# The drain of a software-pipelined retention stage: masks as in every other group, the input added by TensorE, own orders for the last steps

## The chip, the core and the metric

The kernel runs on one core of one Trainium2 chip. A core has TensorE (PE, matmuls, writes PSUM only), VectorE (DVE), ScalarE (ACT), GpSimd (POOL) and SyncE (SP, issues DMAs). They share the on-chip memories SBUF and PSUM, and each runs its own instruction stream; streams wait for one another through semaphores only. The metric is the device time of one launch in microseconds, smaller is better.

## The reference

The input is `x` of shape (1, 2048, 128), float32. Four blocks follow one another, each `x = x + block(layernorm(x))`: a retention network of 4 layers, a mixture of experts, a convolution and cumulative-sum block, and the mixture of experts again. Only the first block is touched. Cut to what matters, with `LN` the layer norm over 128 features and 8 heads of 16 features:

```
X = LN(x)
for i in range(4):
    Z = LN(X)
    Q, K, V, G = rotate(Z @ Wq[i]), rotate(Z @ Wk[i]), Z @ Wv[i], swish(Z @ Wg[i])
    att = (Q @ K.T) * Dm                   # per head, Dm causal with decay
    Y = group_norm(att @ V)
    Yr = (G * Y) @ Wo[i] + X
    X = gelu(LN(Yr) @ W1[i]) @ W2[i] + Yr
x = x + X                                  # the block's residual
```

The mixture of experts that follows starts with `LN(x)`: it needs the mean and variance of each of the 2048 rows of the sum in the last line, and takes an argmax over a projection of the normalised rows.

## The kernel before

**Tiling.** The 2048 rows are 16 chunks of 128; two chunks are a group, so a layer has 8 groups and the four layers have `STEPS` = 32 groups in one sequence (g = 0 to 31). Attention inside a chunk is computed in full and masked with `causal`; what comes from earlier chunks is carried in `state`, which is updated once a chunk (`new_state`). Two tiles hold rows for the whole stage: `xin`, the block's input, and `resid`, the running X (or Yr).

**Pipeline.** The work of a group is spread over eight steps, and each engine runs a loop over t = 0 to 38 (`STEPS + LAG`, LAG = 7). In step t a stage with number n handles group t - n, if there is one (`on(n)`). The stages that matter here:

- n = 0: row statistics, `xz` (normalised rows, ACT L368), turned by PE (L667), copied as `xzT` (ACT L453), projections (PE L715, L725, L727);
- n = 1: rotation (DVE L858, L865, POOL L544), PE turns (L677), ACT copies `qkT` (L446) and `qexp` (L481), PE computes both chunks' scores (L583) into four PSUM banks;
- n = 2: masks. Of each chunk's 8 heads DVE multiplies 4 straight from PSUM (`masked`, L809), and ACT copies the other 4 to SBUF (`raw_scores`, L360), where POOL multiplies them (L524). PE then runs `outputs` (L591 reads `state`, L598), and ACT keeps the result as `yT` (L462);
- n = 3, 4: PE turns `yT` (L612), ACT copies `yc` (L417) and squares it (L439), DVE sums and normalises (L884, L956), PE turns back (L654), ACT makes `ynT` (L430);
- n = 5: DVE multiplies with the gate (`gyT`, L929), PE projects with Wo (L622), DVE adds to `resid` (L972) and takes row statistics (L991);
- n = 6: `xz` again (L368), turned (L667), `xzT` (L453), PE multiplies with W1 (`mlp_up`, L704), ACT makes `hT` (L472);
- n = 7: PE multiplies with W2 (`mlp_down`, L639), DVE adds the product to `resid` (`mlp_added`, L849).

In every step DVE also runs one reciprocal square root for all statistics at once (`rsqrt_steps`, L159 to L182, eight dependent instructions); other DVE instructions are put between its links. It ends in `nmr` (L921), which ACT's L368 waits for.

**Orders.** What each engine does in a step is a list of calls written out by hand, one list for the steps in which the pipeline is full, and one for the drain, the steps in which it runs empty. Before, DVE, PE and ACT take the drain's list from t = 34. In PE's drain list `fill` puts a matmul on constants (L1086, its result is not read) before `mlp_down`, `rows_turned` and `mlp_up`.

**The last group's masks.** For g = 31 DVE masks chunk 0 early in step 33, between the links of the root. For chunk 1 it does all 8 heads itself: L809 for 4, and `masked_rest` (L816) for the other 4, which waits until POOL has masked those of chunk 0, since the same semaphore counts both. ACT and POOL leave chunk 1 of this group out.

**The end of the stage.** From t = 32 on, `block_joined` closes each DVE step: `xin = xin + resid` for a finished group of the last layer (L1002), then `bn_stats` of its two chunks into `next_stats` (L1006). In step 32 it does two groups, then one a step. The next stage's first DVE instruction (L1437) aggregates `next_stats`. ACT also doubles a table of powers in steps 34 to 37 (`tables_doubled` and inside `mlp_hidden`, L2178), work of a later stage.

## Time and profile before

| what | value |
|---|---|
| median of 3 runs | 592.39 us (590.1 to 597.42) |
| the profiled execution's own time | 590.93 us |
| its span, first to last instruction | 589.1 us |
| PE / DVE / ACT / POOL busy | 523.4 / 495.6 / 362.3 / 214.1 us |
| retention stage, its last DVE instruction ends | about 328.9 us |
| next stage, its first DVE instruction | 329.22 us |

The profiled execution is one launch with the hardware profiler on. Its own time holds 1.83 us that lie outside the span. The runs differ among themselves by 7.3 us, so a difference of one or two microseconds is seen in the trace rather than in single times.

### The profile page before, as it was taken

The page shows a single profiled execution, that of the slowest core. Times are in us where ns is not written, and L with a number is a line of the kernel's source. Part 1 is how long each engine was busy: PE and PEld are TensorE (multiplying, and loading weights), DVE is VectorE, ACT ScalarE, POOL GpSimd, SP SyncE. Part 2 cuts the span into 40 slices and gives each one's busy share as a digit, 9 for nine tenths or more (in the row PEclk, how much of TensorE's full clock was granted, in tenths as well). Part 3 has the DMA queues.
Part 4 walks back from the last instruction along what each step waited for, and adds up shares of the span by engine and source line. Part 5 has one row for each costly group of instructions (what it writes and reads, how often), then busy time and mean ns, then how long its engine had stood idle before and what let it go on. Part 6 is the DMA issues. An engine that isn't in the chain of part 4 may idle for free. (4 is left out here: it accounts for less than half of the span.)

```text
span 589.1 us, 13981 instructions
## 1 busy us (share of the span) xinstructions
PE 523.4 (89%) x4372; PEld 409.7 (70%) x4372; DVE 495.6 (84%) x1824; ACT 362.3 (61%) x830; POOL 214.1 (36%) x223
## 2 busy tenths in 40 slices
PE   0788999999999999999968896996499999897994
PEld 0656787878888888888856564994255777456992
DVE  6799999999999999999978897788958999993653
ACT  2577888787888887887747594686144310132760
POOL 2343543543543543543530073474200000072661
PEclk9899999999999999999999999899699999998998
DMA  8979999993000000000000311323000000012315
GB/s 305 364 201 187 182 171 183 181 177 59 3 1 2 2 3 2 2 2 2 2 1 2 116 47 54 87 65 104 0 0 1 2 0 2 0 52 59 101 56 160
DMA packets 61129, 43.29 MB, mean 73 GB/s; under 512 B 4640, under 2 KB 58272, under 8 KB 60800
## 3 DMA queue, kind: packets, MB, share of 16 engines
q1 hardware_dynamic: 56160, 35.42, 30.7%
q0 software_dynamic: 2496, 5.13, 2.6%
q10 hardware_dynamic: 2400, 1.84, 1.0%
q8 instruction: 36, 0.59, 0.5%
q14 instruction: 37, 0.30, 0.2%
HBM read 18.38 MB, written 24.01 MB: 72 GB/s over the span
## 5 line engine op out<-in xcount | busy, mean ns | idle before, releaser
L544 POOL TENSOR_TENSOR qk<-cosq,sinq 128x512 f32<-128x512 f32 x32 | 44.0, 1376 | 164.2 <-DVE cosq L865 164.2
L524 POOL TENSOR_TENSOR att<-att,small 128x512 f32<-128x512 f32 x63 | 79.0, 1275 | 10.2 <-ACT att L360 10.1
L368 ACT ACTIVATE xz<-resid,nmr,rs 128x128 f32<-128x128 f32 x128 | 53.1, 482 | 15.5 <-DVE nmr L921 15.4
L1234 POOL DMA_INDIRECT rows_back<-ffn_yt,ffn_front x46 | 47.8, 1038 | 40.5 <-DVE ffn_yt L1585 36.5
L1414 PE MATMUL banks<-ffn_xtT,ffn_wt 128*128 128x128 f32 x368 | 51.6, 286 | 2.0 <-DVE ffn_hr L1579 2.0
L1414 PEld LDWEIGHTS banks<-ffn_xtT,ffn_wt 128*128 128x128 f32 x368 | 47.1, 200 | 2.8 <-ACT ffn_wt L1261 2.2
L809 DVE TENSOR_TENSOR att<-banks,small 128x512 f32<-128x512 f32 x64 | 43.9, 685 | 4.9 <-PE banks L583 3.9
L1086 PE MATMUL banks<-small 128*128 128x512 f32 (+1 forms) x74 | 31.7, 547 | 13.6 <-POOL osc_taps L1657 11.5
L1225 POOL DMA_INDIRECT rows_in<-ffn_front,ffn_slot x32 | 31.9, 998 | 29.0 <-DVE ffn_slot L1497 20.5
L1217 POOL MEMSET ffn_all_one<- 128x8 f32 x2 | 0.2, 104 | 107.6 <-POOLq L1649 83.8
L360 ACT ACTIVATE att<-banks 128x512 f32<-128x512 f32 x63 | 37.9, 603 | 0.5 <-PE banks L583 0.5
L583 PE MATMUL banks<-qexp,qkT 32*128 32x256 f32 x512 | 36.7, 400 | 1.5 <-ACT qexp L481 1.5
L704 PE MATMUL banks<-xzT,w 128*128 128x256 f32 x128 | 36.2, 405 | 1.0 <-ACT xzT L453 1.0
L715 PE MATMUL banks<-wqkvg,xzT 128*128 128x256 f32 x128 | 35.4, 401 | 1.3 <-ACT xzT L453 1.3
L667 PE MATMUL banks<-small,xz 128*128 128x128 f32 x128 | 21.0, 279 | 17.5 <-ACT xz L368 13.0
L1261 ACT ACTIVATE ffn_wt<-routed_sb 128x512 f32 x46 | 28.8, 630 | 11.6 <-PE banks L1423 8.8
L598 PE MATMUL banks<-att,ve 128*32 128x128 f32 x1024 | 34.8, 276 | 0.3 <-POOL att L524 0.3
L639 PE MATMUL banks<-w,hT 128*128 128x128 f32 x256 | 34.1, 276 | 0.5 <-ACT hT L472 0.5
L639 PEld LDWEIGHTS banks<-w,hT 128*128 128x128 f32 x256 | 31.2, 192 | 1.8 <-ACT hT L472 1.7
L583 PEld LDWEIGHTS banks<-qexp,qkT 32*128 32x128 f32 x512 | 23.1, 184 | 13.1 <-ACT qexp L481 10.5
L472 ACT ACTIVATE hT<-banks 128x512 f32<-128x512 f32 x32 | 19.1, 597 | 20.5 <-PE banks L704 20.5
L1331 PE MATMUL banks<-ffn_xnT,s_gu_sb 128*128 128x512 f32 x64 | 31.1, 605 | 0.4 <-DVE ffn_hs L1523 0.3
(259 smaller groups left out, 1430.5 us busy)
## 6 DMA issues: line engine op xcount, KB each, us to landing
rows_in<-zero_rows SPq DMA_DIRECT2D x16, 1032.0 KB, 19.2
shared_tab<-in_rot SPq DMA_DIRECT2D x3, 1024.0 KB, 12.5
routed_sb<-in_routed SPq DMA_DIRECT2D x1, 3072.0 KB, 12.4
ffn_front<-rows_in SPq DMA_DIRECT2D x46, 64.5 KB, 1.8
ffn_yg<-rows_back SPq DMA_DIRECT2D x8, 256.0 KB, 3.7
shared_tab<-in_rot ACTq DMA_DIRECT2D x1, 1024.0 KB, 10.0
w<-in_W SPq DMA_DIRECT2D x2, 512.0 KB, 7.4
times<-in_times SPq DMA_DIRECT2D x1, 1024.0 KB, 4.9
```

What stands on the lines that cost most here:

```text
L360: act.activation(att[:, c, HALF:HEADS].rearrange("p (r e) n -> p r e n", e=PER_TILE), b_att[:, 2:4, c], ACT.Copy).then_inc(s["att_raw"], 1)
L368: ins = act.activation(xz[:, n], resid[:, (g % GROUPS) * 2 + n % 2], ACT.Identity, scale=rs[:, n:n + 1], bias=nmr[:, n:n + 1])
L524: pool.tensor_tensor(att[:, c, HALF:HEADS], att[:, c, HALF:HEADS], spread(causal.unsqueeze(1), 1, HALF), ALU.mult) \
L544: pool.tensor_tensor(qk[:, v].rearrange("p a b c -> p (a b c)"), cosq[:].rearrange("p a b -> p (a b)"), sinq[:].rearrange("p a b -> p (a b ...
L583: ins = pe.matmul(b_att[:, r, c], qkT[rows, v, 1, c], qexp[rows, v % 2, c], start=True, stop=True)
L598: ins = pe.matmul(b_y[32 * q:32 * q + 32, c * P:c * P + P], ve[:, v, c, q, e].rearrange("p j d -> p (j d)"), att[:, c, 2 * q + e, :], star ...
L639: ins = pe.matmul(b_wq[:, c * P:c * P + P], hT[:, f, c * P:c * P + P], w2[:, layer(g), f, :], start=(f == 0), stop=(f == 1))
L704: ins = pe.matmul(b_xv[:, 256 * f:256 * f + 256], w1[:, layer(g), f * P:f * P + P], xzT[:, 2:4], start=True, stop=True)
L715: ins = pe.matmul(b_wq[:, 256 * c:256 * c + 256], xzT[:, c], wqkvg[:, layer(t), 0:2, :], start=True, stop=True)
L809: dve.tensor_tensor(att[:, c, 0:HALF].rearrange("p (r e) n -> p r e n", e=PER_TILE), b_att[:, 0:2, c], spread(spread(causal.unsqueeze(1).u ...
L1234: pool.indirect_dma_start(rows_back, bass.IndirectOffsetOnAxis(ap=token, axis=0), yt[:, j % RING], None).then_inc(stored[j % RING], 16)
L1414: ins = pe.matmul(banks[:, 2 + v, n * P:n * P + P], wt[:, j % WT_RING, n * P:n * P + P], xtT[:, v], start=True, stop=True)
```

## The change

Five edits, all in the retention stage:

1. The last group is masked like all others: ACT copies and POOL masks four heads of chunk 1, `masked_rest` and `last_masked` are gone.
2. In the last layer (g = 24 to 31) `mlp_down` lets PE add the input: after W2's two matmuls of a chunk a third, the identity times the chunk of `xin`, accumulates on the same PSUM columns. `mlp_added` then writes its sum (PSUM + `resid`) to `xin`. The join L1002 is gone.
3. `block_statistics` takes the statistics of group t - 8, one step after its `mlp_added`, between the links of the root; one call after the loop does the last group.
4. ACT takes the drain's list from t = 32, DVE and PE from t = 33 (all from t = 34 before), and the lists have the calls for the stages that are still on there.
5. Inside the drain's lists the order changes: on DVE the MLP's statistics come before `mlp_added`; on PE `mlp_up` comes before `both_outputs`, and `outputs_turned` before `project`; on ACT the queries by head come before `yT` and `hT`, and both score copies before `yc`.

The diff, cut:

```diff
@@ scalar
                 def second_raw(t, u, on):
-                    if on(2) and t != STEPS + 1:
+                    if on(2):
                         raw_scores(t - 2, 1)
...
                 def step(t, u, on):
-                    if t < STEPS + 2:
+                    if t < STEPS:
                         tables_doubled(t, u, on)
...
                     else:
                         tables_doubled(t, u, on)
                         mlp_rows(t, u, on)
+                        values_copied(t, u, on)
+                        first_raw(t, u, on)
+                        second_raw(t, u, on)
                         outputs_kept(t, u, on)
                         squares(t, u, on)
                         heads_scaled(t, u, on)
+                        qk_copied(t, u, on)
                         rows_copied(t, u, on)
+                        queries_by_head(t, u, on)
+                        outputs_copied(t, u, on)
                         mlp_hidden(t, u, on)
@@ gpsimd
                 def second_masked(t, u, on):
-                    if on(2) and t != STEPS + 1:
+                    if on(2):
                         masked(t - 2, 1)
@@ tensor
                             for f in range(2):
                                 ins = pe.matmul(b_wq[:, c * P:c * P + P], hT[:, f, c * P:c * P + P],
-                                                w2[:, layer(g), f, :], start=(f == 0), stop=(f == 1))
+                                                w2[:, layer(g), f, :], start=(f == 0),
+                                                stop=(f == 1 and g < STEPS - GROUPS))
+                            if g >= STEPS - GROUPS:
+                                ins = pe.matmul(b_wq[:, c * P:c * P + P], eye, xin[:, 2 * (g & (GROUPS - 1)) + c],
+                                                start=False, stop=True)
...
-                    if t < STEPS + 2:
+                    if t < STEPS + 1:
                         outputs_turned(t, u, on)
...
                     else:
+                        outputs_turned(t, u, on)
                         project(t, u, on)
-                        outputs_turned(t, u, on)
                         mlp_down(t, u, on)
                         heads_turned(t, u, on)
                         rows_turned(t, u, on)
                         mlp_up(t, u, on)
+                        both_outputs(t, u, on)
@@ vector
-                def masked_rest(g, c):
-                    wait(dve, s["att_masked_rest"], 2 * g + c)
-                    dve.tensor_tensor(att[:, c, HALF:HEADS].rearrange("p (r e) n -> p r e n", e=PER_TILE),
...
-                    dve.tensor_tensor(x0, b_wq[:, 0:256].rearrange("p (c d) -> p c d", c=2), x0,
+                    dve.tensor_tensor(pair(xin, g) if g >= STEPS - GROUPS else x0,
+                                      b_wq[:, 0:256].rearrange("p (c d) -> p c d", c=2), x0,
                                       ALU.add).then_inc(s["x_next"], 1)
...
+                def block_statistics(t):
+                    g = t - 8
+                    wait(dve, s["x_next"], g + 1)
+                    for c in range(2 * (g - STEPS + GROUPS), 2 * (g - STEPS + GROUPS) + 2):
+                        dve.bn_stats(out_stats[:, c], xin[:, c])
+
+                def block_joined(t, u, on):
+                    if t >= STEPS:
+                        block_statistics(t)
...
-                        for g in ([GROUPS - LAG - 1] if t == STEPS else []) + [GROUPS - LAG + t - STEPS]:
-                            dve.wait_ge(s["x_next"], STEPS - GROUPS + g + 1)
-                            p2 = slice(2 * g, 2 * g + 2)
-                            dve.tensor_tensor(xin[:, p2], xin[:, p2], resid[:, p2], ALU.add) \
-                               .then_inc(s["joined"], 1)
-                            dve.wait_ge(s["joined"], g + 1)
-                            for c in range(2 * g, 2 * g + 2):
-                                dve.bn_stats(out_stats[:, c], xin[:, c])
...
-                    if t < STEPS + 2:
+                    if t < STEPS + 1:
                         row_statistics(t, u, on)
...
                     else:
                         head_variances(t, u, on)
                         aggregated(t, u, on)
+                        first_keys_values(t, u, on)
                         newton = chain_begun(t, on)
                         gated(t, u, on)
                         next(newton)
+                        second_state(t, u, on)
                         next(newton)
                         next(newton)
+                        second_keys_values(t, u, on)
                         next(newton)
+                        block_joined(t, u, on)
                         next(newton)
+                        first_state(t, u, on)
                         next(newton)
                         next(newton)
                         chain_ended(t, newton)
                         means(t, u, on)
                         heads_normalised(t, u, on)
+                        first_scores_masked(t, u, on)
                         projection_added(t, u, on)
+                        second_scores_masked(t, u, on)
+                        mlp_statistics(t, u, on)
                         mlp_joined(t, u, on)
-                        mlp_statistics(t, u, on)
-                        block_joined(t, u, on)
...
                 run(step)(dve)
+                block_statistics(STEPS + LAG)
```

Line numbers differ between the two kernels. Three places of the order, each first before, then changed.

ACT in step 32, from the score copies (L360) to the step's end; `qexp` is what PE's scores of group 31 wait for:

```order
L360 ACTIVATE att<-banks 128x512
L417 ACTIVATE yc<-banks 128x256
L360 ACTIVATE att<-banks 128x512
L430 ACTIVATE ynT<-banks,gn 128x256
L439 ACTIVATE sq<-yc 128x256
L446 ACTIVATE qkT<-banks 128x512
L453 ACTIVATE xzT<-banks,lnsb 128x256
L462 ACTIVATE yT<-banks 128x256
L472 ACTIVATE hT<-banks 128x512
L481 ACTIVATE qexp<-qkT,small 128x2x128 x2
```

```order
L360 ACTIVATE att<-banks 128x512 x2
L417 ACTIVATE yc<-banks 128x256
L439 ACTIVATE sq<-yc 128x256
L430 ACTIVATE ynT<-banks,gn 128x256
L446 ACTIVATE qkT<-banks 128x512
L453 ACTIVATE xzT<-banks,lnsb 128x256
L481 ACTIVATE qexp<-qkT,small 128x2x128 x2
L462 ACTIVATE yT<-banks 128x256
L472 ACTIVATE hT<-banks 128x512
```

`qexp` (L481 before and after) moves from behind `yT` (L462) and `hT` (L472) to in front of both, and `yc` (L417) moves behind the second score copy.

PE in step 33, whole; `banks<-small,yT` turns the outputs, `banks<-w,hT` is `mlp_down`, `banks<-xin,small` the identity times the input, `banks<-xzT,w` is `mlp_up`, and `banks<-qkT,state` with `banks<-att,ve` are the outputs of group 31:

```order
L612 MATMUL banks<-small,yT 128x128 x2
L622 MATMUL banks<-wo,gyT 128x128 x2
L639 MATMUL banks<-w,hT 128x128 x4
L654 MATMUL banks<-small,yc 128x128 x2
L667 MATMUL banks<-small,xz 128x128 x2
L591 MATMUL banks<-qkT,state 128x128 x2
L598 MATMUL banks<-att,ve 32x128 x16
L704 MATMUL banks<-xzT,w 128x256 x2
```

```order
L618 MATMUL banks<-small,yT 128x128 x2
L628 MATMUL banks<-wo,gyT 128x128 x2
L645 MATMUL banks<-w,hT 128x128 x2
L649 MATMUL banks<-xin,small 128x128
L645 MATMUL banks<-w,hT 128x128 x2
L649 MATMUL banks<-xin,small 128x128
L664 MATMUL banks<-small,yc 128x128 x2
L677 MATMUL banks<-small,xz 128x128 x2
L714 MATMUL banks<-xzT,w 128x256 x2
L597 MATMUL banks<-qkT,state 128x128 x2
L604 MATMUL banks<-att,ve 32x128 x16
```

The outputs of group 31 move from in front of `mlp_up` to the step's end, and two matmuls on `xin` are new.

DVE at the start of step 34, from the aggregation to the middle of the root's links (`vv`, `vy`, `vt`):

```order
L892 BN_AGGR mv<-stats 128x2 x2
L1015 TENSOR_SCALAR vv<-mv 128x22
L929 TENSOR_TENSOR gyT<-ynT,gate 128x256
L159 TENSOR_SCALAR vy<-vv 128x22
L162 TENSOR_TENSOR vt<-vy 128x22
L165 TENSOR_TENSOR vt<-vt,vv 128x22
L168 SCALAR_TENSOR_TENSOR vy<-vt,vy 128x22
L172 TENSOR_TENSOR vt<-vy 128x22
```

```order
L897 BN_AGGR mv<-stats 128x2 x2
L1009 TENSOR_SCALAR vv<-mv 128x22
L940 TENSOR_TENSOR gyT<-ynT,gate 128x256
L159 TENSOR_SCALAR vy<-vv 128x22
L839 SCALAR_TENSOR_TENSOR state<-state,small,kvm 128x128
L162 TENSOR_TENSOR vt<-vy 128x22
L165 TENSOR_TENSOR vt<-vt,vv 128x22
L168 SCALAR_TENSOR_TENSOR vy<-vt,vy 128x22
L915 BN_STATS next_stats<-xin 128x6 x2
L172 TENSOR_TENSOR vt<-vy 128x22
```

An update of `state` (L839) and the statistics of group 26 (L915) now stand between the links. The state that this update writes is read by nobody, since group 31 is the last; it still waits until PE has read the first chunk's state in `outputs` of group 31.

## Rows read from the trace of the kernel before

**Rows 1.** The page's part 2: TensorE's granted clock in 40 slices of 14.7 us

```profile
PEclk9899999999999999999999999899699999998998
```

**Rows 2.** Windows: stretch, its length, busy us of each engine, granted clock, DMA

```profile
297.00:304.00 7.00, 3.42 (x33) 2.57 (x27) 4.77 (x14) 2.14 (x6) 3.41 (x16) 1.00 0.00 0
304.00:329.00 25.00, 22.05 (x147) 16.15 (x146) 20.55 (x95) 18.73 (x47) 1.34 (x9) 1.00 0.01 2
```

**Rows 3.** Timeline of DVE, steps 32 and 33: start, length, instruction, [idle before, releaser]

```profile
284.69 0.18 DVE L168 SCALAR_TENSOR_TENSOR vy<-vt,vy 128x22 f32<-128x22 f32 x1
284.81 0.35 DVE L835 SCALAR_TENSOR_TENSOR state<-state,small,kvm 128x128 f32<-128x128 f32 x1
285.08 0.17 DVE L172 TENSOR_TENSOR vt<-vy 128x22 f32<-128x22 f32 x1
...
289.03 0.69 DVE L809 TENSOR_TENSOR att<-banks,small 128x512 f32<-128x512 f32 x1 [0.52 <-PE banks L583]
...
291.97 0.52 DVE L1002 TENSOR_TENSOR xin<-xin,resid 128x256 f32<-128x256 f32 x1
...
293.76 0.40 DVE L884 TENSOR_REDUCE mv<-sq 128x16 f32<-128x256 f32 x1
...
297.58 0.69 DVE L809 TENSOR_TENSOR att<-banks,small 128x512 f32<-128x512 f32 x1 [1.22 <-PE banks L583]
...
298.95 0.17 DVE L921 SCALAR_TENSOR_TENSOR nmr<-mv,rs 128x6 f32<-128x6 f32 x1
...
301.89 0.69 DVE L816 TENSOR_TENSOR att<-banks,small 128x512 f32<-128x512 f32 x1 [1.50 <-POOL att L524]
```

**Rows 4.** Timeline of PE, steps 32 to 37

```profile
289.09 0.61 PE L622 MATMUL banks<-wo,gyT 128*128 128x128 f32 x4
289.54 1.06 PE L639 MATMUL banks<-w,hT 128*128 128x128 f32 x8
...
293.63 1.13 PE L704 MATMUL banks<-xzT,w 128*128 128x256 f32 x4
296.29 1.15 PE L583 MATMUL banks<-qexp,qkT 32*128 32x256 f32 x16 [1.54 <-ACT qexp L481]
...
304.00 1.08 PE L598 MATMUL banks<-att,ve 128*32 128x128 f32 x32
...
310.14 1.13 PE L704 MATMUL banks<-xzT,w 128*128 128x256 f32 x4 [0.34 <-ACT xzT L453]
...
324.42 1.13 PE L704 MATMUL banks<-xzT,w 128*128 128x256 f32 x4 [0.22 <-ACT xzT L453]
```

**Rows 5.** Timeline of ACT, steps 31 to 33

```profile
280.59 0.59 ACT L360 ACTIVATE att<-banks 128x512 f32<-128x512 f32 x1
...
283.47 0.77 ACT L453 ACTIVATE xzT<-banks,lnsb 128x512 f32<-128x512 f32 x1
...
292.30 0.56 ACT L453 ACTIVATE xzT<-banks,lnsb 128x256 f32<-128x256 f32 x1
...
295.35 0.89 ACT L481 ACTIVATE qexp<-qkT,small 128x256 f32<-128x256 f32 x2
...
305.14 0.38 ACT L462 ACTIVATE yT<-banks 128x256 f32<-128x256 f32 x1 [0.33 <-PE banks L598]
306.24 0.60 ACT L472 ACTIVATE hT<-banks 128x512 f32<-128x512 f32 x1 [0.71 <-PE banks L704]
```

**Rows 6.** Timeline of DVE, the last steps and the next stage's first instruction

```profile
322.19 0.17 DVE L921 SCALAR_TENSOR_TENSOR nmr<-mv,rs 128x6 f32<-128x6 f32 x1
...
327.50 0.42 DVE L849 TENSOR_TENSOR resid<-banks,resid 128x256 f32<-128x256 f32 x1 [1.37 <-PE banks L639]
327.96 0.42 DVE L1002 TENSOR_TENSOR xin<-xin,resid 128x256 f32<-128x256 f32 x1
328.42 0.49 DVE L1006 BATCH_NORM_STATS2 next_stats<-xin 128x6 f32<-128x128 f32 x2
329.22 1.17 DVE L1437 BATCH_NORM_AGGREGATE ffn_mv<-next_stats 128x2 f32<-128x6 f32 x16 [0.31 <-PEq L307]
```

More of the change, by code:

```diff
@@ L278, in retention @@
             "var_ready", "bn_stats_done", "bn_aggr_done", "rs_chain", "rs_ready", "nmr_ready", "xz_ready",
-            "yn_ready", "gy_ready", "yr_ready", "x_next", "joined")}
+            "yn_ready", "gy_ready", "yr_ready", "x_next")}
         N_FIRST, N_W, N_ROT = 6, 7, 3
@@ L812, in masked @@
                                       ALU.mult).then_inc(s["att_masked"], 1)
-                def masked_rest(g, c):
-                    wait(dve, s["att_masked_rest"], 2 * g + c)
-                    dve.tensor_tensor(att[:, c, HALF:HEADS].rearrange("p (r e) n -> p r e n", e=PER_TILE),
-                                      b_att[:, 2:4, c],
-                                      spread(spread(causal.unsqueeze(1).unsqueeze(1), 1, 2), 2, PER_TILE),
-                                      ALU.mult).then_inc(s["att_masked_rest"], 1)
                 def chunk_decay(g, c):
@@ L908, in second_keys_values @@
                         keys_values(t - 2, 1)
-                def last_masked(t, u, on):
-                    if t == STEPS + 1:
-                        masked(t - 2, 0)
                 def first_state(t, u, on):
@@ L960, in first_scores_masked @@
                     if on(2):
-                        if t == STEPS + 1:
-                            masked(t - 2, 1)
-                            masked_rest(t - 2, 1)
-                        else:
-                            masked(t - 2, 0)
+                        masked(t - 2, 0)
                 def projection_added(t, u, on):
@@ L983, in second_scores_masked @@
                 def second_scores_masked(t, u, on):
-                    if on(2) and t != STEPS + 1:
+                    if on(2):
                         masked(t - 2, 1)
@@ L993, in mlp_statistics @@
                         ins.then_inc(s["bn_stats_done"], 1)
-                def block_joined(t, u, on):
-                    if isinstance(t, int) and t >= STEPS:
-                        for g in ([GROUPS - LAG - 1] if t == STEPS else []) + [GROUPS - LAG + t - STEPS]:
-                            dve.wait_ge(s["x_next"], STEPS - GROUPS + g + 1)
-                            p2 = slice(2 * g, 2 * g + 2)
-                            dve.tensor_tensor(xin[:, p2], xin[:, p2], resid[:, p2], ALU.add) \
-                               .then_inc(s["joined"], 1)
-                            dve.wait_ge(s["joined"], g + 1)
-                            for c in range(2 * g, 2 * g + 2):
-                                dve.bn_stats(out_stats[:, c], xin[:, c])
                 def chain_begun(t, on):
@@ L1041, in step @@
                         next(newton)
+                        block_joined(t, u, on)
                         second_keys_values(t, u, on)
-                        last_masked(t, u, on)
                         first_state(t, u, on)
@@ L1065, in step @@
                         next(newton)
+                        second_state(t, u, on)
                         next(newton)
                         next(newton)
+                        second_keys_values(t, u, on)
                         next(newton)
+                        block_joined(t, u, on)
                         next(newton)
+                        first_state(t, u, on)
                         next(newton)
@@ L1074, in step @@
                         heads_normalised(t, u, on)
+                        first_scores_masked(t, u, on)
                         projection_added(t, u, on)
+                        second_scores_masked(t, u, on)
+                        mlp_statistics(t, u, on)
                         mlp_joined(t, u, on)
-                        mlp_statistics(t, u, on)
-                        block_joined(t, u, on)
                 run(step)(dve)
+                block_statistics(STEPS + LAG)
 def keep_running(pe, bank, consts, n, cols=512):
```

## The prediction

> **What bounds the kernel now.** I read the clock line first. All slices from 103 to 295 us and the drain's stand near full speed; only later ones fall, the lowest at 412 us [rows 1]. In the drain, 297 to 329 us, the granted clock is 1.00, so its matmuls run at the higher level, 2.4 GHz [rows 2]. The chain of waits reaches back only to 504 us, so the drain has to be read from the timelines.
>
> Three things stand there. First the hand-over at group 31: from 297 to 304 us PE is busy 3.42 us of 7, DVE 4.77 [rows 2]. Its scores start at 296.29, after 1.54 us of idle PE, released by ACT's `qexp` [rows 4]; DVE's mask waits 1.22 us for them, and later 1.50 us for POOL, because the one counter must pass chunk 0 first [rows 3]. Second the joins: step 32 does two, 1.79 us from 291.97 to 293.76 [rows 3]. Third the tail: the last product's sum starts at 327.50 after 1.37 us of waiting for PE, then the join, the statistics, and the next stage at 329.22 [rows 6]. Nothing but this DVE row opens the next stage, 0.31 us after the last statistics, so what the drain's end gains is passed on whole.
>
> **The change part by part**, as shifts of the profiled execution. Times of after are worked out.
>
> 1. *The identity pair.* Two 128x128 matmuls a step, g = 24 to 31. Nearest row: the two of Wo, 289.09 to 289.54 start to start [rows 4], 0.45 us. In steps 31 and 32 PE is continuous up to the rotation's turn, which itself waits for the MLP sum behind the pair, so both pairs push everything back: **+0.9**.
>
> 2. *Joins and statistics of step 32.* DVE loses 1.79 us; step 33 starts at 293.76 + 0.89 - 1.79 = 292.86, **0.9 earlier**. One statistics pair comes back between the links, about 0.35 us, ahead of a mask that waits 0.52 us for scores [rows 3]: nothing. Without that cover it would cost its 0.35.
>
> 3. *`qexp` forward on ACT.* Before, `xzT` ends at 292.86, then `yT` and `hT` wait for PE, and `qexp` runs at 295.35 for 0.89 [rows 5]. Now it follows `xzT`: 292.86 + 0.89 + 0.89 = 294.6. PE is then still in `mlp_up` (293.63 + 0.89 + 0.97 = 295.5, its 1.13 less 0.16 of overlap), so the scores of group 31 start at 295.5, **0.8 earlier** than 296.29 [rows 4], the 1.54 us of idle gone.
>
> 4. *Step 33 on DVE.* Before, first row to `nmr` took 5.19 us (293.76 to 298.95), of which 1.22 idle and 0.61 mask [rows 3]. Now 3.36 + 0.36 (`gyT`, moved ahead) + 0.33 (statistics), so `nmr` at 296.9, 2.0 earlier. An instruction put between two links costs less than its length: `state` takes 0.35, yet the links around it start 0.39 apart against 0.21 without it, so 0.18 [rows 3]. The masks follow without waiting. The 1.50 us and L816 go, ACT and POOL take them over: POOL's second mask ends near 300.9, before PE needs it.
> The Trainium skill, "VectorE: DVE Perf Modes", The DRAIN you can't avoid, says that the next instruction does not start until the pipe has emptied, excepting ones not held back, and advises counting instructions. By its first half each of the five insertions of step 33 would cost its full length, 1.9 us where I count 1.3, and the gain would be 0.6 smaller, if nothing hid it. The row speaks against that half here, since `state` starts 0.12 us after a link 0.18 long.
>
> 5. *Outputs of group 31.* They now stand behind `mlp_up`, which waits for `xzT`. ACT has, from 297.07: two `xz` (0.8), the two score copies, `yc`, the squares, `ynT`, then `xzT`. The same run in step 31, from the first score copy to `xzT`, took 2.88 us for six starts [rows 5], of which 0.5 is a `qkT` copy that step 33 lacks. That gives 300.1 for `xzT`, 300.6 for `mlp_up`, 301.6 for the state reads, 302.1 for L598 in place of 304.00 [rows 4]: **1.9 earlier**. PE idles 1.5 us ahead of `mlp_up`. `yT` follows at 303.3 and `hT` right behind it at 303.6, where it was 306.24 [rows 5]: 2.6 earlier, though `hT` could have had its product at 301.8. PE then turns, projects and fills (1.15), `mlp_down` from 304.8 with its pair 1.34, turn, fill, turn 0.9, `xzT`, fill, and the next `mlp_up` at 307.9 against 310.14 [rows 4]: **2.2 earlier**.
>
> 6. *The useless `state` update of step 34* waits until PE reads the state at 301.6 and holds DVE for about 1.0 us. `nmr` comes at 304.1, when ACT ends `hT`, also 304.1: nothing, but by a hair.
>
> 7. *Steps 35 to 37.* Before, the three periods from 310.14 to 324.42 [rows 4] take 14.28 us, DVE being nearly always busy (20.55 of 25 us over the drain [rows 2]). Each DVE step loses its join, 0.46 us (327.96 to 328.42 [rows 6]), so DVE stops being the limit; the ring PE, ACT takes over: `mlp_up` to `hT` 1.2, `hT` 0.65, `mlp_down` with its pair 1.34, turns and fill 0.7 to 0.9, `xzT` and fill 1.0, or 4.85 a step with heads turned and about 4.75 without. Three take 14.5: the last `mlp_up` starts at 322.4, **2.0 earlier** than 324.42.
>
> 8. *The tail.* 3.08 us from that `mlp_up` to the last sum [rows 4, 6], plus 0.45 for the pair, less 0.46 for the join: 0.
>
> **Sum:** the next stage starts at 327.2 instead of 329.22, **-2.0 us**. The profiled execution of 590.93 becomes 588.9. It lies 1.5 below the median of the runs; I set the forecast on the middle between the two, 591.7, which gives **589.7 us**. Bounds: with both insertions and pair wholly hidden, -3.5; with the insertions at full length and the last pair uncovered, -1.0.
>
> **The rivals.**
>
> *More of it passes on.* By item 4 DVE ends step 33 near 299.5, 4.9 us ahead of 304.4. If ACT and PE returned their parts faster than I count, for instance because the 1.5 us of idle PE in item 5 closes and the ring of item 7 keeps the old 4.76 us, about 4 us would reach the end: 587.7. Against it: items 5 and 7 are bound by a serial ring in which every piece has a row.
>
> *The ring costs more than the waits it replaces (the other side).* Place: step 33, outputs behind `mlp_up`, `hT` behind `yT`. What was parallel, PE's outputs beside ACT's copies, is now in series. If the copies of ACT ahead of `xzT` must wait once more, say for PE's turn that waits for DVE's projection sum, a whole ACT run of 2.4 to 2.9 us [rows 5] is added: -2.0 + 2.6 = +0.6, 592.3. It decides from the point where L598 starts 2.0 us later than the 302.1 of item 5, at 304.1. For it: DVE and ACT meet within 0.3 us in items 5 and 6. Against: PE reaches the heads' turn at 298.6, after the sum that it needs, 298.2.
>
> *The clock falls.* PE idles about 1.5 us near 299 and 0.6 near 303. Before, PE was idle 1.54 us ahead of 296.29 [rows 4] and 3.6 of the 7 us from 297 on, and the clock stayed at 1.00 [rows 2]. If it fell to 1.2 GHz for some 5 us of the drain, PE, busy 22.05 of 25 us [rows 2], would lose up to 5, and the sum would be +3: 594.7.
> The Trainium skill, "TensorE: Matmul & The Clock Gate", The HAM clock gate, says that PE's default is the low clock and that idleness brings it back. By that rule this rival is real, but the same rows show the clock holding through more idleness than I expect.
>
> *Nothing reaches the end.* ACT's last table or PE's last fill could close the stage: 591.7. Against it, ACT's last copy comes 2 us before DVE's end, and both move with the same ring.
>
> **How the numbers follow.** The forecast gets 0.58, more passing on 0.15, the costlier ring 0.13, nothing 0.1, the clock 0.04. Predicted 589.7. The range 586.8 to 593.2 takes in the bounds -3.5 and -1.0, most of the first two rivals and the median's scatter (single runs spread over 7 us), and leaves out the clock and the tails. A difference of 2%, 11.8 us, is about what a measurement of this kernel can tell from no change; no case comes near it, the whole retention drain being 32 us long. So within 2%: 0.98, faster 0.01, slower 0.01.
>
> **What would show it.** Scores of group 31 at 0.8 us earlier, with no idle from `qexp`; the first DVE row of step 33 at 0.9 earlier; PE idle about 1.5 us ahead of `mlp_up` in step 33 and its outputs behind it near 302; DVE idle about 1.0 us at the `state` update; `hT` directly behind `yT`; then DVE waiting in each step for `mlp_down`, where it waited 0.2 to 0.5 us; the next stage at about 327.2. The prediction is wrong if the last steps' period falls below 4.6 us, if the identity matmul starts are not 0.22 us apart, or if anything past 330 us changes its length.

## The result, and the profile after

Times are medians of 20 executions each, taken by turns on one chip.

| | before | changed |
|---|---|---|
| median | 592.54 us | 589.91 us |
| lowest to highest | 590.1 to 597.42 | 587.02 to 593.37 |
| profiled execution | 590.93 (span 589.1) | 589.88 (span 588.1) |
| ratio | | 0.9964, 95% interval 0.9949 to 0.998 |

The changed kernel is faster by 0.36%, about 2.1 us, within the 2% that count as no change. The forecast was 589.7.

Where the two profiles are compared, one offset has to go first: group 29's scores, which stand ahead of all that the change acts on, start at 278.91 us before and at 279.74 in the changed kernel, 0.83 later. From that row to the next stage's first instruction, called **the stretch** below, before took 50.31 us and the changed kernel 47.88: **2.43 less**, where -2.0 had been worked out.

Windows of the changed kernel, with the columns of [rows 2]:

```profile
297.00:304.00 7.00, 5.73 (x74) 4.67 (x66) 6.29 (x23) 3.82 (x10) 4.95 (x19) 1.00 0.00 0
304.00:329.00 25.00, 22.86 (x134) 17.61 (x135) 17.57 (x96) 18.82 (x46) 1.50 (x12) 1.00 0.01 1
```

In the hand-over PE is busy 5.73 us of 7 where it was 3.42, DVE 6.29 where it was 4.77. After it DVE is busy 17.57 us where it was 20.55: it no longer sets the pace (E3 and E11 below show it). Timeline of PE, which answers to [rows 4]:

```profile
296.41 1.15 PE L589 MATMUL banks<-qexp,qkT 32*128 32x256 f32 x16
...
298.65 0.39 PE L649 MATMUL banks<-xin,small 128*128 128x128 f32 x2
298.88 0.61 PE L645 MATMUL banks<-w,hT 128*128 128x128 f32 x4
...
301.15 1.13 PE L714 MATMUL banks<-xzT,w 128*128 128x256 f32 x4 [1.00 <-ACT xzT L453]
302.12 0.61 PE L597 MATMUL banks<-qkT,state 128*128 128x128 f32 x4
302.65 1.08 PE L604 MATMUL banks<-att,ve 128*32 128x128 f32 x32
304.24 0.44 PE L618 MATMUL banks<-small,yT 128*128 128x128 f32 x2 [0.50 <-ACT yT L462]
...
308.42 1.13 PE L714 MATMUL banks<-xzT,w 128*128 128x256 f32 x4 [0.22 <-ACT xzT L453]
...
322.83 1.13 PE L714 MATMUL banks<-xzT,w 128*128 128x256 f32 x4 [0.22 <-ACT xzT L453]
```

The scores (L589) have no idle time before them, where 1.54 us stood. Each of the two L649 starts 0.23 us ahead of the operation behind it. The outputs (L597, L604) stand behind `mlp_up` (L714), which waits 1.00 us for `xzT`. Timeline of DVE, which answers to [rows 3, 6]:

```profile
293.69 0.40 DVE L889 TENSOR_REDUCE mv<-sq 128x16 f32<-128x256 f32 x1
...
297.41 0.17 DVE L932 SCALAR_TENSOR_TENSOR nmr<-mv,rs 128x6 f32<-128x6 f32 x1
...
300.82 0.87 DVE L1009 TENSOR_SCALAR vv<-mv 128x22 f32<-128x22 f32 x1
...
302.65 0.37 DVE L839 SCALAR_TENSOR_TENSOR state<-state,small,kvm 128x128 f32<-128x128 f32 x1 [0.39 <-PE banks L597]
...
326.36 0.43 DVE L853 TENSOR_TENSOR xin<-banks,resid 128x256 f32<-128x256 f32 x1 [2.23 <-PE banks L649]
326.82 0.49 DVE L915 BATCH_NORM_STATS2 next_stats<-xin 128x6 f32<-128x128 f32 x2
327.62 1.17 DVE L1437 BATCH_NORM_AGGREGATE ffn_mv<-next_stats 128x2 f32<-128x6 f32 x16 [0.31 <-PEq L307]
```

And of ACT, which answers to [rows 5]; `hT` follows `yT` at once:

```profile
294.03 0.56 ACT L453 ACTIVATE xzT<-banks,lnsb 128x256 f32<-128x256 f32 x1
294.48 0.90 ACT L481 ACTIVATE qexp<-qkT,small 128x256 f32<-128x256 f32 x2
...
303.80 0.38 ACT L462 ACTIVATE yT<-banks 128x256 f32<-128x256 f32 x1 [2.71 <-PE banks L604]
304.08 0.59 ACT L472 ACTIVATE hT<-banks 128x512 f32<-128x512 f32 x1
305.11 0.88 ACT L368 ACTIVATE xz<-resid,nmr,rs 128x128 f32<-128x128 f32 x2 [0.44 <-DVE nmr L932]
```

**Past the drain.** Of the 1.60 us by which the next stage starts earlier in these two profiles (329.22 to 327.62), 0.96 are left at 503 us (L1086 at 504.24 and 503.28). Windows of the changed kernel just behind the drain, then the same of before:

```profile
333.62:335.62 2.00, 2.00 (x10) 1.20 (x10) 1.69 (x10) 0.69 (x2) 0.00 (x0) 0.68 0.35 84
335.62:337.62 2.00, 2.00 (x9) 1.72 (x9) 1.35 (x7) 0.00 (x0) 0.00 (x0) 0.50 0.00 0
```

```profile
333.62:335.62 2.00, 1.31 (x11) 1.12 (x11) 1.93 (x8) 0.60 (x1) 0.00 (x0) 1.00 0.95 284
335.62:337.62 2.00, 1.87 (x12) 1.04 (x11) 1.72 (x9) 0.69 (x2) 0.00 (x0) 1.00 0.18 45
```

In the second window the granted clock is at the lower level (0.50) in the changed kernel's profile. Two products (L1331) take 1.92 us there, 1.02 before, and POOL's first gather starts 10.95 us after the stage's first row (338.57) instead of 10.32 (339.54): 0.6 us given back in this execution. Not every profile shows this: E1 and E2 below show the low clock at this place too (gather 10.75 and 11.09 us after the first row), E3 to E7 and E11 don't (10.32 or 10.33), and E7 is the changed kernel but for one update. What decides it stays open.

### The profile page after: what moved, and what is told of

Its sections match the earlier page's. It is cut to its first block and busy times, and to the rows that moved or that the text cites. A ratio compares the mean times of both kernels' runs of the same rounds, so it can differ in the third digit from the quotient of the medians.

```text
span 588.1 us, 14041 instructions
## 1 busy us (share of the span) xinstructions
PE 528.0 (90%) x4404; PEld 414.8 (71%) x4404; DVE 493.4 (84%) x1816; ACT 362.9 (62%) x831; POOL 214.6 (36%) x224
## 5 line engine op out<-in xcount | busy, mean ns | idle before, releaser
L530 POOL TENSOR_TENSOR att<-att,small 128x512 f32<-128x512 f32 x64 | 80.3, 1275 | 6.7 <-ACT att L360 6.7
L1086 PE MATMUL banks<-small 128*128 128x512 f32 (+1 forms) x74 | 31.7, 547 | 13.1 <-POOL osc_taps L1657 11.5
L360 ACT ACTIVATE att<-banks 128x512 f32<-128x512 f32 x64 | 38.3, 603 | 0.2 <-PE banks L589 0.2
L714 PE MATMUL banks<-xzT,w 128*128 128x256 f32 x128 | 36.2, 405 | 1.9 <-ACT xzT L453 1.9
L589 PE MATMUL banks<-qexp,qkT 32*128 32x256 f32 x512 | 36.7, 400 | 0.0
L645 PE MATMUL banks<-w,hT 128*128 128x128 f32 x256 | 35.5, 276 | 0.5 <-ACT hT L472 0.5
L604 PE MATMUL banks<-att,ve 128*32 128x128 f32 x1024 | 35.0, 276 | 0.5 <-POOL att L530 0.5
L1331 PE MATMUL banks<-ffn_xnT,s_gu_sb 128*128 128x512 f32 x64 | 31.9, 619 | 0.4 <-DVE ffn_hs L1523 0.3
L472 ACT ACTIVATE hT<-banks 128x512 f32<-128x512 f32 x32 | 19.1, 597 | 19.8 <-PE banks L714 19.8
L1579 DVE TENSOR_TENSOR ffn_hr<-ffn_silr,banks 128x256 f32<-128x256 f32 x46 | 19.3, 420 | 14.1 <-ACT ffn_silr L1303 9.6
```

Source lines behind the costliest of these rows:

```text
L360: act.activation(att[:, c, HALF:HEADS].rearrange("p (r e) n -> p r e n", e=PER_TILE), b_att[:, 2:4, c], ACT.Copy).then_inc(s["att_raw"], 1)
L530: pool.tensor_tensor(att[:, c, HALF:HEADS], att[:, c, HALF:HEADS], spread(causal.unsqueeze(1), 1, HALF), ALU.mult) \
L589: ins = pe.matmul(b_att[:, r, c], qkT[rows, v, 1, c], qexp[rows, v % 2, c], start=True, stop=True)
L645: ins = pe.matmul(b_wq[:, c * P:c * P + P], hT[:, f, c * P:c * P + P], w2[:, layer(g), f, :], start=(f == 0), stop=(f == 1 and g < STEPS - ...
L714: ins = pe.matmul(b_xv[:, 256 * f:256 * f + 256], w1[:, layer(g), f * P:f * P + P], xzT[:, 2:4], start=True, stop=True)
L1086: pe.matmul(bank[:, 0:cols], consts[:, 0:P], consts[:, 0:cols], start=True, stop=True)
```

## The experiments

E1 to E4 ran on one chip and E5 to E8 on another, on which the kernel before takes 620.84 and 621.01 us, E9 to E12 on a third, where it takes 592.17. So ratios to the kernel before of the same chip are compared, and the stretch of each profile. All times but the ratio are counted from the start of group 29's scores and come from one profile each. Where the outputs have two times, PE waits for a mask between the first chunk's and the second's; elsewhere both chunks run without a break:

| kernel | group 31's scores | its outputs | last `mlp_up` | stretch | ratio (95%) |
|---|---|---|---|---|---|
| before | 17.38 | 25.09 | 45.51 | 50.31 | 1 |
| changed | 16.67 | 22.91 | 43.09 | 47.88 | 0.9964 (0.9949 to 0.998) |
| E1 join on DVE | 15.85 | 22.60 | 42.46 | 47.25 | 0.9923 (0.9894 to 0.9953) |
| E2 outputs first | 16.67 | 20.78, 21.87 | 41.94 | 46.73 | 0.994 (0.991 to 0.997) |
| E3 no fill | 16.67 | 22.91 | 42.34 | 47.13 | 0.9928 (0.9887 to 0.997) |
| E4 masks only | 17.38 | 21.18, 22.35 | 43.12 | 47.92 | 0.9947 (0.9923 to 0.9972) |
| E5 = E2 + E3 | 16.66 | 20.78, 21.87 | 41.20 | 45.99 | 0.9913 (0.9885 to 0.994) |
| E6 = E1 + E5 + E7 | 15.84 | 20.38, 21.56 | 41.93 | 46.72 | 0.993 (0.9898 to 0.9963) |
| E7 no dead update | 16.66 | 22.90 | 43.07 | 47.86 | one run |
| E8 own counter | 17.38 | 25.22 | 46.21 | 51.01 | 0.9995 (0.9968 to 1.0021) |
| E9 = E8 again | 17.39 | 25.23 | 45.95 | 50.75 | one run |
| E10 = before again | 17.39 | 25.95 | 46.36 | 51.16 | one run |
| E11 = E4 + E3 | 17.39 | 21.18, 22.34 | 43.11 | 47.91 | 0.9966 (0.9939 to 0.9993) |
| E12 all but masks | 16.67 | 28.83 | 49.57 | 54.36 | 1.0103 (1.0072 to 1.0134) |

**E1.** The changed kernel without the identity product; DVE joins between the chain's links, ahead of the statistics.

```
-  if g >= STEPS - GROUPS: ins = pe.matmul(b_wq[...], eye, xin[...], start=False, stop=True)
+  dve.tensor_tensor(xin[:, p2], xin[:, p2], resid[:, p2], ALU.add).then_inc(s["joined"], 1)
```

> The changed kernel, but PE's identity matmuls are gone and DVE joins input and result again, inside the statistics call one step later. Measured in the trace from the start of group 29's scores to the next stage's first aggregation: 50.3 us before, 47.9 changed. Theory (the drain is a serial ring of PE and ACT, and the identity pair lies on it): the pairs of steps 31 and 32 give back 0.9, the ring of steps 34 to 37 shrinks from 4.75 to 4.3 a step, DVE with its join (about 4.8 a step) becomes the limit again, so not all of the pairs is won: 45.5, that is 4.8 us less than before. Rival (taking the join off DVE is what gained): the join costs its 0.46 us in each drain step and the stretch is 48.5 or more.

Both missed: the stretch is 47.25, between 45.5 and 48.5. The scores came 0.82 earlier, so the pair's +0.9 in two steps is right. Of that only 0.63 arrived. In steps 34 to 36 DVE has no wait once the `state` update is done, so it sets the pace again: a period from `mlp_up` to `mlp_up` that took 4.95 in the changed kernel takes 5.38. The last two wait for PE and take 4.54 and 4.47 for 4.73. One of the steps without a wait, 4.61 us from `vv` to `vv`:

```profile
311.89 0.18 DVE L1010 TENSOR_SCALAR vv<-mv 128x22 f32<-128x22 f32 x1
...
313.19 0.42 DVE L913 TENSOR_TENSOR xin<-xin,resid 128x256 f32<-128x256 f32 x1
...
316.50 0.18 DVE L1010 TENSOR_SCALAR vv<-mv 128x22 f32<-128x22 f32 x1
```

**E2.** PE's outputs of group 31 ahead of `mlp_up` in the drain, as before the change.

```
-  mlp_up(t, u, on)
   both_outputs(t, u, on)
+  mlp_up(t, u, on)
```

> The changed kernel with one swap: in the drain's list PE runs the outputs ahead of the MLP's up product. Theory (in step 33 PE idles 1.0 us ahead of the up product and 0.5 ahead of the turn, because the outputs stand behind it and ACT's yT comes late): the outputs start near 0.1 us after the rows' turn, wait for POOL's second mask, yT comes 1.2 earlier, and the ring moves 0.9 to 1.1 earlier: stretch 46.9 against 47.9. Rival (POOL's second mask is late, so PE waits for it with the up product stuck behind): hT is later by the 1.0 us that the up product loses, stretch 48.4.

Met: the stretch is 46.73, 1.15 shorter. The outputs of the first chunk start 2.13 us earlier; those of the second wait for POOL's mask, and `yT` starts 1.48 earlier. So the order that item 5 prices costs 1.15 us, with nothing given back.

**E3.** The changed kernel without PE's filler matmul (`fill(t)`, 0.60 us) ahead of `rows_turned`.

> The changed kernel without the filling matmul ahead of the MLP rows' turn in steps 34 to 38. Theory (PE's part of the ring is on the path): in steps 36 and 37 the fill's 0.43 us falls on the path and comes back; in steps 34 and 35 ACT copies the heads' turn first, which hides it; in all 1.0 us, stretch 46.9, granted clock still 1.00. Rival (the fills are what keeps the clock): the granted clock falls below 1.00 in the drain and the stretch is over 48.5. Second rival (ACT bounds the ring): stretch unchanged at 47.9.

The stretch is 0.75 us shorter, 47.13 where 46.9 was expected, most of it in the last two periods (4.29 and 4.54 where they were 4.73 each). The granted clock stays at 1.00 up to the next stage, so both rivals are out. PE does set the pace there, as item 7 has it.

**E4.** The kernel before with the first edit alone.

```
-  if on(2) and t != STEPS + 1:      (ACT's copy, POOL's mask, DVE's second mask)
+  if on(2):
-  masked(t - 2, 1); masked_rest(t - 2, 1)      (and last_masked's masked(t - 2, 0))
+  masked(t - 2, 0)
```

> The kernel before with only the first edit: the last group is masked like all others. Theory: the two waits of DVE in step 33 (1.22 and 1.50 us) and both masks' delay go; the up product of group 27 starts 3.4 us earlier, DVE starts step 34 3.1 us earlier and stays the limit as before, so the stretch is 47.2, as good as the whole change or better. Rival (own orders and the PE addition are needed for the gain): only the 1.5 us wait goes and the next wait takes the rest, stretch 48.8.

The masks alone give 2.39 of the 2.43 us, 0.7 less than expected. POOL, one mask after the other, is now what PE waits for between the two halves of the outputs:

```profile
298.59 2.51 POOL L524 TENSOR_TENSOR att<-att,small 128x512 f32<-128x512 f32 x2 [6.45 <-ACT att L360]
```

```profile
299.99 0.64 PE L598 MATMUL banks<-att,ve 128*32 128x128 f32 x16
301.16 0.64 PE L598 MATMUL banks<-att,ve 128*32 128x128 f32 x16 [0.52 <-POOL att L524]
```

But DVE sets the pace of this kernel, as E11 shows, and it is DVE that comes late: it starts step 34 only 2.51 us earlier (23.01 for 25.52), not 3.1. It waits for `mlp_down`, and its join takes 0.84 us instead of 0.44 (the row stands in the last section):

```profile
299.22 0.42 DVE L849 TENSOR_TENSOR resid<-banks,resid 128x256 f32<-128x256 f32 x1 [0.47 <-PE banks L639]
```

E4 keeps the outputs first, as E2 does. E2 is E4 with the identity pair, the moved statistics and the new orders but that one, and is 1.19 us shorter. So with the masks in place the other edits gain 1.19 and lose 1.15 through the outputs' order.

**E5.** E2 and E3 together.

> The changed kernel with both edits that shortened the ring: PE's outputs ahead of the up product in the drain, and no filling matmul ahead of the MLP rows' turn. They gained 1.15 and 0.75 us alone (stretch 46.7 and 47.1 against 47.9). Theory (both lie on the same serial ring of PE and ACT, at different places): they add, stretch 46.0. Rival (DVE or ACT's table work is next in line right behind): less than 0.4 of the second is left, stretch 46.4 or more. Clock in the drain 1.00 in both.

The two add, and this is the shortest: 4.32 us off the stretch of before, 1.89 off the changed kernel's. By the ratios, whose intervals overlap, it is not told from E1 to E4; against the changed kernel's 0.9964 from another chip its interval lies below.

**E6.** E1 with both edits of E5 and without the dead `state` update.

> The same two ring edits on the version that joins on DVE and has no identity matmuls (stretch 47.25 alone), and without the useless last update of the state. Theory (that version is bound by DVE in steps 34 and 35 and by the ring only in 36 and 37): outputs first gives what the state stall held, 0.6 to 1.0, the fill gives about 0.3 since DVE is behind it, stretch 46.1, no better than the identity version. Rival (the identity pair is pure cost): 45.6 or less.

Missed by both. With PE's ring shortened DVE's is the longer (no wait from step 34 on, until the last two), so the join belongs on PE: with it 45.99, without 46.72. E1 and E6 together show where the identity product pays: it costs 0.63 us while the outputs stand behind `mlp_up` and the fill is in, and saves 0.73 once both are gone.

**E7.** The changed kernel without the `state` update of step 34 (`if on(3) and t - 3 < STEPS - 1`).

> The changed kernel without the update of the state in step 34 that nobody reads. Theory (its stall on DVE is covered: PE's down product with its pair ends later than the rows need it): DVE no longer idles 0.39 us there, stretch unchanged at 47.9 (within 0.1). Rival (the stall holds the normalised rows and with them the ring): stretch 47.3 to 47.5.

Met: 0.02 us. ACT no longer waits for `nmr` and starts `xz` 0.57 us sooner than in the changed kernel (24.80 for 25.37), but PE turns it no sooner (27.63 for 27.64), being busy with `mlp_down`, its pair and the fill:

```profile
304.12 0.87 ACT L368 ACTIVATE xz<-resid,nmr,rs 128x128 f32<-128x128 f32 x2
...
306.95 0.38 PE L677 MATMUL banks<-small,xz 128*128 128x128 f32 x2
```

**E8.** The kernel before; DVE's last eight-head mask waits for ACT's copy only, on the other counter.

```
-  wait(dve, s["att_masked_rest"], 2 * g + c)
+  wait(dve, s["att_raw"], 2 * g + c)
...      (its end counts on att_masked, and PE waits for that)
```

> The kernel before, where DVE's eight-head mask of the last chunk no longer waits for POOL's mask of the other chunk: it counts on another semaphore and waits only for ACT's copy out of the same bank. Nothing else changes. Theory (the 1.50 us of DVE waiting for POOL is on the path, and the early mask's wait of 1.22 us is what masking like all others gains beyond it): the mask starts 1.3 earlier, stretch 49.0 against 50.3. Rival (PE or ACT end the next wait at about the same time): stretch 49.8 or more.

Missed by both: the wait of 1.50 us shrank to 0.15, and the mask started 1.35 earlier, but the stretch was 0.7 longer and the time the same.

```profile
301.62 0.69 DVE L819 TENSOR_TENSOR att<-banks,small 128x512 f32<-128x512 f32 x1 [0.15 <-ACT att L360]
```

In its profile the clock was low (0.70 from 298 to 302 us, 0.50 from 302 to 306). E9 is the same program once more, E10 the kernel before once more.

> The kernel before with the last eight-head mask on a counter of its own, the same program once more. In its first profile the granted clock fell to 0.70 and 0.50 between 298 and 306 us, and the drain took 51.01 us from group 29's scores to the next stage. Theory (the fall belongs to that one execution): clock 1.00 in the drain, mask 1.35 us earlier than in the kernel before, and 49.0 to 49.5 us. Rival (the edit itself brings the fall): the clock is below 1.00 between 298 and 306 us again, and the drain takes about 51 us.

> The kernel before, unchanged, in one more profiled execution on this chip. Theory (no clock fall in its drain, as in its first profile): 50.3 us from group 29's scores to the next stage, clock 1.00. Rival (its hand-over at group 31 is just as exposed): the clock falls between 298 and 306 us here too, and the drain takes 52 to 54 us.

The rival came true for E9. Of E10's rival the fall came true, but the drain took 51.16 us and not 52 to 54. Windows of E9, one of E10, then PE's rows of E10 and of E9:

```profile
298.00:302.00 4.00, 2.21 (x17) 1.67 (x10) 3.17 (x9) 1.63 (x4) 0.46 (x1) 0.62 0.00 0
302.00:306.00 4.00, 4.00 (x39) 3.73 (x42) 2.92 (x13) 1.32 (x3) 4.00 (x23) 0.53 0.02 4
```

```profile
298.00:302.00 4.00, 2.87 (x12) 2.64 (x12) 2.35 (x8) 1.63 (x4) 1.88 (x8) 0.50 0.00 0
```

```profile
295.83 1.15 PE L583 MATMUL banks<-qexp,qkT 32*128 32x256 f32 x16 [1.54 <-ACT qexp L481]
...
299.13 1.20 PE L622 MATMUL banks<-wo,gyT 128*128 128x128 f32 x4 [1.79 <-DVE gyT L929]
300.12 1.92 PE L639 MATMUL banks<-w,hT 128*128 128x128 f32 x8
```

```profile
300.56 1.19 PE L625 MATMUL banks<-wo,gyT 128*128 128x128 f32 x4 [1.79 <-DVE gyT L932]
301.54 1.92 PE L642 MATMUL banks<-w,hT 128*128 128x128 f32 x8
```

The kernel before has the fall too, in some executions: after 1.54 and 1.79 us of idle PE its products take 1.20 and 1.92 us, where `mlp_down` took 1.06 at full clock [rows 4]. It costs before 0.85 us of the stretch (51.16 against 50.31). Of E8 no profile without the fall was seen, so what its 1.35 us are worth at full clock stays open; at the low clock, 0.15 to 0.41 (51.01 and 50.75 against 51.16).

This bears on the main result. Of the five profiles that mask group 31 as before (before, E8, E9, E10, E12) four show the fall in the drain; of the nine that mask it like the others (changed, E1 to E7, E11) none does. So the 2.43 us are measured against before's better case; against E10 they would be 3.28. How often the runs without a profile fell is not known.

**E11.** E4 without the filler matmul of E3.

> The kernel before with group 31's masks as the others', and without PE's fill ahead of the rows' turn. Theory (with the joins still on DVE, DVE sets the pace of the last steps, so PE's fill is hidden): 47.7 to 47.9 us of drain, as with the masks alone (47.92), and the same time as the version with the masks alone, ratio to the kernel before 0.995. Rival (the fill lies on the ring there too): 47.2 us, as it gave 0.75 us in the changed kernel.

The theory holds: 47.91 against 47.92. The fill is worth 0.75 us where PE sets the pace and nothing where DVE does.

**E12.** The changed kernel with the masks of group 31 as before.

> The changed kernel with group 31's masks put back to what the kernel before does (DVE masks chunk 0 in the chain of step 33, then both parts of chunk 1; ACT and POOL leave them out). Theory (the masks' edit holds the gain, the identity pair, the moved statistics and the new orders cancel one another): 50.0 to 50.7 us from group 29's scores to the next stage, ratio to the kernel before 0.999 to 1.001. Rival (the other edits hold a gain of their own that the masks' edit only overlaps): 48.5 to 49.2 us, ratio 0.997.

Both missed: the stretch is 54.36, 3.7 us above the upper end of what the theory gave, and the time is 1.0% longer. DVE and PE of E12 at the hand-over:

```profile
297.61 0.69 DVE L820 TENSOR_TENSOR att<-banks,small 128x512 f32<-128x512 f32 x1 [1.75 <-PE banks L589]
...
302.70 0.69 DVE L827 TENSOR_TENSOR att<-banks,small 128x512 f32<-128x512 f32 x1 [1.83 <-POOL att L530]
```

```profile
303.77 0.69 PE L664 MATMUL banks<-small,yc 128*128 128x128 f32 x2 [4.15 <-DVE resid L990]
304.25 0.64 PE L677 MATMUL banks<-small,xz 128*128 128x128 f32 x2
305.62 2.07 PE L714 MATMUL banks<-xzT,w 128*128 128x256 f32 x4 [0.73 <-ACT xzT L453]
307.49 1.06 PE L597 MATMUL banks<-qkT,state 128*128 128x128 f32 x4
308.48 1.63 PE L604 MATMUL banks<-att,ve 128*32 128x128 f32 x32
```

The mask stands between the chain's links and waits for the scores, so `nmr` comes at 299.76. ACT copies the scores behind `xz`, which needs `nmr`; POOL masks after the copy, DVE's last mask after POOL, the projection's sum after that, and PE's turn after the sum: it idles 4.15 us. The kernel before has this chain too, and it is no shorter there: counted from group 29's scores, PE's turn (L654 before, L664 here) starts at 24.05 before and at 24.12 in E12.

The loss comes behind the turn. With `mlp_up` ahead of the outputs, PE waits for `xzT` and then does `mlp_up` first, and the outputs start at 28.83 where they started at 25.09. `hT` follows `yT` at 30.82 where it was 27.33. And the clock has fallen: `mlp_up` takes 2.07 us, and from its start to `yT` (310.19) it is 4.57 us where the changed kernel needs 2.65 (301.15 to 303.80). So some 1.9 of the 4.05 us are the low clock, an estimate from these rows. The profile is one of E12's longer executions, 599.49 in a range from 594.36 to 599.74.

So the edits are not a sum of parts. Without the masks' edit the other four cost 4.05 us against the first profile of before, and 3.2 against E10's, which has the low clock too; with it they are worth 0.04. That the order of the outputs alone makes the loss is read from the rows: E12 with the outputs first was not run.

## Why the prediction was right

The forecast case came true by its own steps: -2.43 us in the stretch where -2.0 was worked out. That the median of 589.91 lies only 0.2 from the 589.7 is partly luck. The forecast set out from 591.7 for the kernel before, whose median came out at 592.54, and the gain was larger than forecast, so the two misses nearly cancel. With 0.83 us taken off the times of the changed kernel:

| step | worked out | measured |
|---|---|---|
| 2: first DVE row of step 33 | 292.86 | 292.86 |
| 3: scores of group 31 | 295.5 | 295.58 |
| 4: `nmr` of step 33 | 296.9 | 296.58 |
| 5: `xzT` | 300.1 | 299.71 |
| 5: `mlp_up` | 300.6 | 300.32 |
| 5: outputs | 302.1 | 301.82 |
| 5: `hT` | 303.6 | 303.25 |
| 5: next `mlp_up` | 307.9 | 307.59 |
| 7: last `mlp_up` | 322.4 | 322.00 |
| next stage | 327.2 | 326.79 |

**Items 1 to 3** held to 0.1 us; E1 gives the pair its 0.8.

**Item 4** was mis-sized by 0.3 us, and nearly all of the total miss of 0.4 stems from it. From the first row of step 33 to `nmr` it took 3.72 us (293.69 to 297.41) where 4.05 was said. The five insertions, by how much the links around them moved apart from their usual 0.21, cost 0.34 (`gyT`), 0.28 (the statistics) and 0.13 to 0.15 each (two `state`, one `kvm`): 1.0 us, not 1.3. The Trainium skill, "VectorE: DVE Perf Modes", The DRAIN you can't avoid, has a rule, weighed there, that would have cost each its full length (1.9 us), and an exception for instructions that are not held back. The trace agrees with the exception: `state` starts at 295.03, 0.08 after the start of a link 0.17 long.

**Item 5**: PE idled 1.00 us ahead of `mlp_up` where 1.5 was said, 0.3 of it for the same reason. From `nmr` to the next `mlp_up` it took 11.01 us where 11.0 was said. On the way the terms given for `xzT` (297.07, 0.8, and 2.88 less 0.5) add up to 300.25, not 300.1. The order itself was priced rightly but not questioned: E2 shows that it loses 1.15 us.

**Item 6**: 0.39 us of waiting, not 1.0. DVE came later by 0.7 because `vv` took 0.87 instead of 0.17. The verdict, nothing, was right, but not by the cover that it names. `nmr` did not come before `hT` had ended: ACT stood 0.44 us waiting for it (`xz` at 305.11). What covers the stall is PE, which turns these rows only at 307.38; in E7 they are ready 0.57 us sooner and nothing comes of it.

**Item 7**: the three periods took 4.95, 4.73 and 4.73, or 14.41 for 14.5. That is better than its parts. As listed (1.2, 0.65, 1.34, 0.7 to 0.9, 1.0) they add up to 4.9 to 5.1 a step, not to 4.75 and 4.85. Measured in the last step they are 1.17, 0.65, 1.44, 0.65 and 0.82: the pair's part was set too short and the last one too long. Added rightly, they would have put the last `mlp_up` near 322.9, so the small miss here is luck as well. E3 and E11 show that PE's ring is the bound in the changed kernel and DVE's in the kernel with the masks alone.

**Item 8** held: from the last `mlp_up` to the next stage it is 4.79 us, 4.80 before.

**The rivals.** "The ring costs more" decides from outputs at 304.1; they came at 301.82. The same order, outputs behind `mlp_up` and `hT` behind `yT`, is where E12 loses: there they come at 28.83 on the count from group 29's scores, which is 307.74 on this scale. "Nothing reaches the end" is excluded by the next stage's start. "The clock falls" was wrong for the drain of the changed kernel, but its argument against, that before holds the clock through more idleness, rested on one execution, and E10 shows that it doesn't always. One of the prediction's own signs of being wrong did appear: past 330 us two products take 1.92 us instead of 1.02, since the clock is low there, and 0.6 us is lost in that profile. E7's profile doesn't show it, so it need not come with the change.

What the prediction did not say is which edit gains. It read as if all contributed; E4 shows the first alone giving 2.39 of 2.43.

## What to carry to other kernels

Orders, waits and covers of one hand-over are priced together: an edit that yields all the gain alone (E4) can be the condition under which the others are harmless (E12). Before an addition moves from one engine to another, read which engine's ring sets the period after all the other edits, since the same join is worth -0.73 or +0.63 us (E5 against E6, changed against E1). Where a profile shows the full clock across idle gaps of 1.5 us, look at a second execution before calling the stretch safe.

## What the runs showed of the hardware

**A short DVE operation beside POOL's masks takes up to the rest of the mask longer.** `vv`, a TENSOR_SCALAR 128x22, takes 0.17 us at 294.40, and 0.17 to 0.18 in all its other 23 rows between 100 and 310 us of the changed kernel's profile, none of them beside a mask. At 300.82 it took 0.87 and ended at 301.69, just behind POOL's pair of masks:

```profile
299.06 2.50 POOL L530 TENSOR_TENSOR att<-att,small 128x512 f32<-128x512 f32 x2 [5.30 <-ACT att L360]
```

In E4, whose pair ended at 301.10, the join met it instead:

```profile
300.55 0.84 DVE L997 TENSOR_TENSOR xin<-xin,resid 128x256 f32<-128x256 f32 x1
```

In E11, of the same orders, it takes 0.83 at this place. E4's five later joins take 0.41 to 0.43, with no mask beside them. In both, the statistics that ran beside the same POOL operation kept their lengths, and so did the sum (L853, 0.42 at 299.75), which takes one operand from the matmul banks. The Trainium skill, "SBUF — State Buffer", SBUF: two separate sides, says that DVE and POOL share a pair of ports as an exclusive lock, for DVE in a two-port mode or with two inputs from SBUF, and that the loser waits for the whole instruction; the trace agrees for these two. In E12, where POOL masks one chunk only and is done at 302.66, `vv` takes 0.18 (305.08), but no run changed the POOL operation alone.

**The clock after idle gaps differs between executions** of one program: 1.00 and 0.50 in before's 298 to 302 us (its first profile and E10), after the same waits of 1.54 and 1.79 us.
